# First-layer aggregation products moved into the build of the adjacency, one per step, with six PSUM banks for the steps

## The reference

```python
# layer 0: attention-like, with a sigmoid weight per edge
Q, K, V = h @ w_q, h @ w_k, h @ w_v                     # 8 heads of 16
scores = sum(Q[src] * K[dst], per head) * SCALE * sigmoid(sum(edge_attr))
out = segment_sum(V[dst] * scores, dst) / max(count(dst), 1)
x = x + out @ w_o + b_o
# layer 1: x + relu(segment_sum(h[src], dst) @ W_rel.T + b + h @ W_root.T)
# layer 2: two rounds with segment_sum(h[src] * edge_weight, dst), then a linear map
# layer 3: attention with a softmax over the edges of each destination
```

## Time and profile before

| | |
|---|---|
| median of three runs | 7598.0 us (7587.34 to 7602.8) |
| the profiled execution, its span | 7610.71 us, 7608.9 us |
| TensorE busy | 5794.5 us, 76% |
| VectorE busy | 3770.1 us, 50% |
| ScalarE busy | 2412.7 us, 32% |
| GpSimd busy | 1974.2 us, 26% |
| layer products, line 1117 | 19208 records, 2256.2 us |
| step products, line 1082 | 14112 records, 1924.2 us |
| ScalarE's copies, line 922 | 4704, 1657.8 us |
| VectorE's line 1548 | 2352, 1648.9 us |
| stores adj<-field | 882 of 800 KB, 5.1 us to landing |
| loads field<-adj | 196 of 3200 KB, 10.0 us to landing |

### The profile page before, as it was taken

One profiled execution on the slowest core, in us unless ns is written; L12 is line 12 of the kernel. 1 busy time (PEld: TensorE's weight loads), 2 busy tenths in 40 slices (PEclk: granted clock), 3 DMA queues, 4 the chain that ended last, 5 costly groups with the idle time before them and its releaser, 6 DMA issues.

```text
span 7608.9 us, 163268 instructions
## 1 busy us (share of the span) xinstructions
PE 5794.5 (76%) x48472; PEld 4915.9 (65%) x48472; DVE 3770.1 (50%) x7617; ACT 2412.7 (32%) x7276; POOL 1974.2 (26%) x1782
## 2 busy tenths in 40 slices
PE   1777777777777779999999999996256565556665
PEld 1555555555555569999999999996234444444444
DVE  6899999999999962221111111112143333333333
ACT  2666666666666641111110000002022222122222
POOL 2000000000000000000000000003777777777772
PEclk9899899999989989999999999997677777777776
DMA  6666666766766787676676666672222222222221
GB/s 192 278 282 279 282 276 279 288 276 276 285 275 277 285 291 271 258 277 259 276 278 276 277 278 276 278 279 68 49 56 55 55 55 58 56 55 56 55 55 32
DMA packets 260966, 1542.23 MB, mean 203 GB/s; under 512 B 56235, under 2 KB 86965, under 8 KB 233836
## 3 DMA queue, kind: packets, MB, share of 16 engines
q1 hardware_dynamic: 201380, 1406.77, 47.2%
q0 software_dynamic: 59008, 129.85, 7.1%
q10 hardware_dynamic: 130, 0.80, 0.0%
HBM read 795.75 MB, written 743.08 MB: 202 GB/s over the span
## 4 chain that ended last, share of the span: by engine, by line
PE 51%; DVE 20%; issue 11%; POOL 7%; ACT 4%; ACTq 3%; DMA 2%; DVEq 0%; SPq 0%; POOLq 0%
PE psum L1117 29%; DVE field L1548 11%; PE psum L1082 7%; POOL field L809 7%; PE psum L1284 5%; PE psum L1306 5%; ACT field L922 2%; ACTq L907 2%; ACT field L1013 1%; DVE field L1541 1%; DVE work L1843 1%; DVE work L1847 1%; DMA field<-head_table,cmp 1%; DVE field L1542 1%; PE psum L1304 1%
## 5 line engine op out<-in xcount | busy, mean ns | idle before, releaser
L1117 PE MATMUL psum<-field 128*128 128x128 f32 x19208 | 2256.2, 277 | 24.6 <-issue 19.1
L1117 PEld LDWEIGHTS psum<-field 128*128 128x128 f32 x19208 | 2233.3, 189 | 25.3 <-issue 20.2
L1082 PE MATMUL psum<-field 128*128 128x200 bf16 (+1 forms) x14112 | 1924.2, 281 | 132.8 <-DVE field L1548 114.9
L922 ACT COPY field<-psum x4704 | 1657.8, 416 | 958.8 <-PE psum L1082 665.2
L809 POOL DMA_INDIRECT field<-head_table,cmp x1563 | 1644.7, 1052 | 476.7 <-issue 456.8
L1548 DVE TENSOR_TENSOR field<-field 128x1176 bf16<-128x1176 bf16 x2352 | 1648.9, 761 | 0.0
L1082 PEld LDWEIGHTS psum<-field 128*128 128x128 bf16 x14112 | 1077.2, 101 | 425.7 <-issue 159.1
L1073 PE MATMUL psum<-zero_b 128*128 128x2 bf16 x4704 | 807.6, 172 | 456.2 <-ACT field L922 447.8
L1073 PEld LDWEIGHTS psum<-zero_b 128*128 128x128 bf16 x4704 | 478.4, 102 | 643.5 <-issue 578.9
L753 POOL DMA_INDIRECT field<-tile_rows,step_t_i x74 | 201.2, 2719 | 2405.7 <-PE psum L1053 2355.4
L1013 ACT COPY field<-psum x1611 | 433.6, 269 | 1029.6 <-PE psum L1306 718.6
(11 more groups left out here) (289 smaller groups left out, 2720.0 us busy)
## 6 DMA issues: line engine op xcount, KB each, us to landing
adj<-field SPq DMA_DIRECT2D x882, 800.0 KB, 5.1
field<-adj SPq DMA_DIRECT2D x196, 3200.0 KB, 10.0
field<-head_table,cmp POOLq DMA_INDIRECT x1563
field<-in_edge_attr SPq DMA_DIRECT2D x4, 3072.0 KB, 28.5
head_table<-field SPq DMA_DIRECT2D x7, 476.0 KB, 3.2
tile_rows<-field SPq DMA_DIRECT2D x1, 3328.0 KB, 21.0
right_edges<-zeros SPq DMA_DIRECT2D x1, 3328.0 KB, 19.9
place_rows<-right_edges SPq DMA_DIRECT2D x25, 128.0 KB, 2.8
```

The costliest lines, as they stand in the source:

```text
L922: act.copy(evac[:, :, bass.ds(place, SEG)], build_banks[:, bass.ds(bank, NSEG * SEG)].rearrange("p (w c) -> p w c", w=NSEG)).then_inc(pair ...
L1082: mm = pe.matmul(build_banks[:, bass.ds(cur[j % ROUND], end - first)], hot, pr[:, first:end], start=False, stop=True, skip_group_check=True)
L1117: mm = pe.matmul(ps_y[slot][:, 0:D], source[:, hi, :], adj_in[slot][:, :, 2 * hi:2 * hi + 2], start=(hi == 0), stop=(hi == NB - 1))
```

## The change

- The aggregation of layer 0, Y = A h, is taken apart from the rest of the layer. Behind step 14 + hi of chunk c (c from 26 on, hi from 0 to 48) TensorE does one product of block c - 26: `sum_part`. This goes for all whole chunks, so for blocks 0 to 46; blocks 47 and 48 follow the build.
- The sum needs a bank of its own, `ps_y0`: the steps have six banks, and at an even step TensorE waits for copies up to the second-last step. The products of the two count columns go to the same bank.
- Each array is kept as two of 50 columns (block columns 0 to 24; 25 to 48 and the two count columns): a round is stored by six transfers of half the size. SP loads half 1 of a block behind a chunk's first round, half 0 of the next block behind its third. The halves go to the first 25 blocks of X, which are loaded again from the input later, and to the work buffer.
- ScalarE copies a block's sums to Y at the end of the chunk. Y takes H2's place; H and H2 are exchanged.
- The loads of `src_t` and `dst_t` come after the last step instead of at the beginning.
- The rest of layer 0 is `finish()`: in seven groups of seven blocks instead of block by block.
- The later layers load a block in two transfers. L1's third load waits for the stored tables and for all blocks of `finish()`.

```diff
-BUILD_BANKS = 7
+BUILD_BANKS = 6
+TAB_BANK = 7
+L0_CHUNK = 26
+L0_LOOP = L0_CHUNK // PER_LOOP
+Y_FIRST = 14
...
+            def load_half(b, h):                                   # SP
+                at = b * HALF_COLS + HALF
+                rows_d = adj[SIGMOID * HALVES2 + h]
+                sp.wait_ge(half_summed[h], b + HALF0)
+                sp.dma_start(half_flat[h], rows_d[:, at:at + HALF_COLS] ...).then_inc(half_loaded[h], 16)
...
-                        for i in range(NSEG):
-                            sp.dma_start(adj[i].rearrange("p (s c) -> p s c", c=SEG)[:, bass.ds(base[r], ROUND), :]
+                        for i in range(ARRAYS):
+                            sp.dma_start(adj[i].rearrange("p (s c) -> p s c", c=HALF)[:, bass.ds(base[r], ROUND), :]
...
+                        if summing and rc == 0:
+                            load_half(chunk - L0_CHUNK, 1)
+                        if summing and rc == 2:
+                            load_half(chunk - (L0_CHUNK - 1), 0)
...
+            sp.wait_ge(half_summed[0], BLOCKS + HALF0)
+            sp.dma_start(X[:, 0:X_SPOILT, :], x[0:X_SPOILT * P, :].rearrange("(b p) f -> p b f", p=P)).then_inc(x_reloaded, 16)
...
+            pool.wait_ge(step_added, BSTEPS + ADDED0)              # GpSimd: src_t, dst_t only now
...
+            def copy_sums(b):                                      # ScalarE
+                act.wait_ge(half_summed[1], b + (1 + HALF0))
+                act.copy(one(Y, b), ps_y0).then_inc(y_copied, 1)
...
+                    if at == CHUNK - 1 and summing:
+                        copy_sums(k * PER_LOOP + (slot - L0_CHUNK))
...
+            def sum_part(b, hi):                                   # TensorE
+                h, at = half_of(hi)
+                if hi == 0:
+                    pe.wait_ge(y_copied, b + DONE0)
+                if at == 0:
+                    pe.wait_ge(half_loaded[h], b * 16 + 16)
+                mm = pe.matmul(ps_y0[:, 0:D], H[:, hi, :], half_in[h][:, :, at:at + 2], start=(hi == 0), stop=(hi == NB - 1),
+                               skip_group_check=True)
+                if hi == NB - 1:
+                    for i in range(2):
+                        mm = pe.matmul(ps_y0[0:BPAIRS, D + i:D + i + 1], half_in[h][:, :, HALF - 2 + i], ones[:, 0:1], start=True, stop=True)
+                if hi == NB - 1 or half_of(hi + 1)[0] != h:
+                    mm.then_inc(half_summed[h], 1)
...
                     mm.then_inc(step_added, 1)
+                    if summing and slot * CHUNK + CHUNK <= n and Y_FIRST <= at < Y_FIRST + NB:
+                        sum_part(k * PER_LOOP + (slot - L0_CHUNK), at - Y_FIRST)
...
+            def finish():                                          # TensorE; turn: 7 transposes of H, queries: 7 products Y W_q,
+                ...                                                # values: 7 products with W_k and 7 with W_v
+                turn(0)
+                queries(0)
+                values(0)
+                for g in range(GROUPS):
+                    pe.wait_ge(fin_vs_ready, g + 1)
+                    for j in range(GROUP):
+                        mm = pe.transpose(cols(ps[0], j), cols(fin_vs, j), ident[:, :])
+                    mm.then_inc(fin_turned, 1)
+                    pe.wait_ge(fin_turn_copied, 2 * g + 2)
+                    for j in range(GROUP):
+                        mm = pe.matmul(cols(ps[1], j), cols(fin_vsT, j), W["o"], start=True, stop=True)
+                    mm.then_inc(fin_products, 1)
+                    if g + 1 < GROUPS:
+                        turn(g + 1)
+                        values(g + 1)
+                        queries(g + 1)
+                pe.wait_ge(fin_out_taken, GROUPS)
+            for hi in range(NB):
+                sum_part(BLOCKS - 2, hi)
+            pe.wait_ge(y_copied, BLOCKS - 1 + DONE0)
             tables()
-            blocks_of(L0)
+            for hi in range(NB):
+                sum_part(BLOCKS - 1, hi)
+            finish()
             starts()
...
+            finish()                                               # VectorE: per group scores (4 operations, 3 of 128x896), then
+                                                                   # sums (2 of 128x896, 7 bn_stats, 7 bn_aggr), then scale
```

More of the change, by code:

```diff
@@ L30 @@
 NSEG = 3
+HALVES2 = 2
+HALF = SEG // HALVES2
+HALF_HI = HALF // 2
+ARRAYS = NSEG * HALVES2
 ROUND = 16
@@ L91 @@
 PASSES = 2
-L0, L1, L2A, L2B = range(4)
-LAYER_SEG = (SIGMOID, COUNTED, WEIGHTED, WEIGHTED)
-LAGS = (2, 1, 1, 1)
+L1, L2A, L2B = range(3)
+LAYER_SEG = (COUNTED, WEIGHTED, WEIGHTED)
+LAGS = (1, 1, 1)
+LAYERS = 3
 CRING = 3
@@ L956, in body @@
                         stage_block(0, 0)
-                    if layer == L0 and 1 <= j <= NB:
-                        act.wait_ge(kvq_ready, n)
-                        act.copy(kv[ring(layer, j, 1)], ps_kv).then_inc(kv_copied, 1)
                     if j < NB:
@@ L974, in body @@
                         stage_block(b + 1, j + 1)
-                    if layer == L0 and 1 <= j <= NB:
-                        act.wait_ge(vs_turned, n)
-                        act.copy(vsT[ring(layer, j, 1)], ps_v).then_inc(vsT_copied, 1)
                 over_blocks(act, layer, body)
-            for layer in range(4):
+            finish()
+            for layer in range(LAYERS):
                 blocks_of(layer)
-            act.wait_ge(hT_copied, 4 * NB + DONE0)
+            act.wait_ge(hT_copied, LAYERS * NB + DONE0)
             act.wait_ge(block_written, 2 * NB)
@@ L1034, in _ @@
             pe.sem_inc(y_summed, SUMMED0)
+            for h in range(HALVES2):
+                pe.sem_inc(half_summed[h], HALF0)
             pe.wait_ge(consts, CONSTS)
@@ L1229, in _ @@
+            for hi in range(NB):
+                sum_part(BLOCKS - 2, hi)
+            pe.wait_ge(y_copied, BLOCKS - 1 + DONE0)
             tables()
-            blocks_of(L0)
+            for hi in range(NB):
+                sum_part(BLOCKS - 1, hi)
+            finish()
             starts()
-            for layer in (L1, L2A, L2B):
+            for layer in range(LAYERS):
                 blocks_of(layer)
@@ L1370, in _ @@
             c.then(dve.tensor_scalar(tri[:, :], iota[:, :], pidx[:, 0:1], None, ALU.is_gt))
-            c.then(dve.memset(build_banks, 0.0))
+            c.then(dve.memset(psum[:, :], 0.0))
             dve.wait_ge(loaded_edges, 16 * 9)
@@ L1658, in output @@
                     dve.wait_ge(o_ready, m + 1)
-                    if layer == L0:
-                        c.then(dve.tensor_tensor(one(X, b), one(X, b), ps_o, ALU.add))
-                        dve.sem_inc(o_taken, 1)
-                        c.then(dve.tensor_tensor(one(X, b), one(X, b), bias["o"][:, :], ALU.add))
-                        normalise(c, m, norm_b[s], b)
-                    elif layer == L1:
+                    if layer == L1:
                         c.then(dve.tensor_tensor(lin[s], ps_o, bias["rel"][:, :], ALU.add))
@@ L1704, in body @@
                     n = b + layer * NB
-                    if layer == L0 and 1 <= j <= NB:
-                        scores(c, n, b - 1, ring(layer, j, 1))
                     if lag <= j:
```

346 lines of the change are left out of this document (227 added, 119 removed).

## The result

The changed kernel takes 7652.0 us (median of four runs, 7649.3 to 7662.3) against 7592.8 for the kernel before beside it (four runs, 7587.3 to 7602.8): 1.0078 times, 95% interval 1.0066 to 1.0091. It is slower, by 0.8%, clear of the spread of the runs; 7294 was forecast, with a range of 7200 to 7470. The traces differ by 38.5 us and the medians by 59: the profiled execution of the kernel before lies 18 us above its median.

The account below looks back on a forecast made before the run. The prediction took TensorE to bound the layers and VectorE the build. Saving 478 us at the layer, adding 169 for the build and 5 for six banks, gave -304: 7294 us from a median of 7598.0, range 7200 to 7470.

Parts of the forecast that it names:

- Bound: Whole kernel: layers bound by TensorE, build by VectorE (92% busy), with an idle fifth of TensorE for the moved products.
- A pass of two chunks, after: Build loop with products: 78.7 us a pass, 39.4 a chunk, 3.6 more than before; 47 chunks make +169 us.
- upper bound of 46.8 us a chunk: Build chunk with products at 0.38 us each: 49 x 0.146 more, +517 us in all.
- Product: Each summing product moved into the build takes TensorE 0.234 us, as in the later layers; bounds nothing and 0.38.
- Six banks: Build steps with six banks for seven: copies waited for one later, +5 us, range 0 to 112.
- The DMA queue: Build: 13.1 MB a chunk takes 31.1 us of 39.4 at 422 GB/s, so half loads and stores stay hidden.
- rival 2: Build: transfers become the pace through late stores, 43.8 us a chunk, +207 us, 7501 us in all; chance 0.13.
- The layer: Last build step to next layer's first product: 187 us for 665, saving 478; finish() 18 us a group; bounds 150 and 240.
- X reload: Between build and next layer: a late reload of X, 1.6 MB, adds 5 us.
- Three layers for nothing: The three layers behind: two loads per block for one cost nothing, as their TensorE is full.
- Rival 4: Build: stalls keep TensorE's clock low through half the product stretch, 12.8 us a chunk, +600, 7894 us; chance 0.07.
- Rival 5: Build: chunk 10.1 us longer instead of 3.6, products near 0.36 us, giving back all saved, 7598 us; chance 0.02.

Follow-up runs that it names:

- e6_act_one: Changed kernel with one chunk per loop pass instead of two on TensorE and ScalarE, in chunks with and without products; 7397.8 us, 0.9753 of the kernel before.
- e13_one_no_products: e6_act_one without the build's 47 x 49 summing products, loads kept; one run, no ratio given, a pass of two chunks 79.5 us.
- e15_late_x: e6_act_one with one half's buffer moved to the last half of X, its reload waited for before the fourth group of finish(); 0.9783 of the kernel before.
- e5_one_chunk: Changed kernel with one chunk per pass instead of two in TensorE's summing loop only, all products kept; 0.9990 of the kernel before.

## Why the prediction was wrong

**Bound.** Right: the layers were TensorE's, the build VectorE's, and TensorE's idle fifth could be used. What I read as one stall for ScalarE was a fetch of ScalarE's instructions, and so a thing that grows with traffic.

**A pass of two chunks, after: the step that failed.** 78.7 us forecast, 89.4 measured; 47 chunks made +416, not +169. Of the 17.7 us more than before:
- 4.5 are fetches: 89.4 - 81.2 = 8.2 us a pass in the changed kernel, 71.7 - 68.0 = 3.7 before. In both, steps at the low clock behind the stall are part of it (clock 0.95, and 0.99 with short loops). I had kept the 3.8 of the earlier trace rows and never asked whether TensorE's body still stayed where it was after 49 more products a chunk. It didn't: 8.26 us, beside ScalarE's.
- 13.2 are the work itself, 68.0 to 81.2 with short loops, where 7.1 were forecast. 98 x (0.600 - 0.569) = 3.0 of the difference is the product: 0.26 us and not 0.234. The distance of its columns doesn't explain that and its neighbours at most in part; it stays open. The other 3 I can't divide. The transfers aren't seen in them, as half the loads take nothing off; but relieving TensorE alone helps no more, for without any product a pass still takes 79.5 us.

The upper bound of 46.8 us a chunk was mis-added: 39.4 + 49 x 0.146 is 46.5, and +504 us. The measured 44.6 lies below it; the range, which ended at 7470, stopped short of both.

The Trainium skill (Advanced Engine Details and Errata, ISA Cache) gives TensorE's instruction cache as 128 KB and the other engines' as 32 KB, in lines of 16 KB. The traces agree with these sizes: with the long bodies a pass brought TensorE nine packets of 16 KB, 147 KB, and ScalarE five of 8 KB, 41 KB; halved, an estimated 74 and 21 KB, the bodies weren't fetched at all (no packet from 1200 to 2600 us in e6_act_one). In the size of a packet the trace agrees for TensorE (1.47 MB/90 = 16 KB) and not for ScalarE (0.48 MB/59 = 8 KB). No run shows at which length fetching starts.

**Product.** 0.234 taken, 0.26 measured, within the bounds of 0 and 0.38.

**Six banks.** 5 taken, some 17 left for them in the chunks without products, none with short loops.

**The DMA queue, "hidden".** Wrong, but not by itself decisive: rival 2's mechanism shows once the products are gone, and hardly with them. It gave 43.8 us for a chunk paced by stores; without products the chunk took 43.1, or 39.7 with short loops. That a queued load would fill a store's start-up didn't hold: 13.1 MB in 39.7 us are 330 GB/s, with the engines 91% busy, where I had reckoned with the 422 of the earlier trace rows. That row is of stores alone. The Trainium skill's limit of about 358 GB/s for a core (DMA: Bandwidth & Descriptors, Specifications), weighed in the prediction and set aside, was the better guide for stores and loads together: no window of 1500 us with both passes it. In windows of 2 us the trace of e13_one_no_products does, with up to 419 GB/s.

**The layer.** Right: 201.7 us against 187, with 20.5 us a group of finish() for 18 (two of VectorE's sums start at 3322.78 and 3343.30). The X reload took 31.3 us where 5 were added, and cost little by luck: e15_late_x shows that only some 5 us of the wait stood alone.

**Three layers for nothing.** Wrong: +90.4 us. I had asked whether their second load was hidden, and it is; the operand's distance, 50 floats for 100, I hadn't asked about at all. Had only this failed, the forecast would still have had its sign (-304 + 90); had only the build failed (+254 in the table), it would have kept it too, with -50. It took both.

**Rival 4, the clock.** It didn't come: 0.95 over the product chunks, above the 0.91 of the earlier trace rows. In the product chunks the clock is low behind the jump's stall, and with short loops it reads 0.99. In the kernels without products, where TensorE idles more, it reads 0.82 and 0.87: e13_one_no_products falls to 0.53 or less five times between 1904 and 1984 us, behind idle times of up to 2.3 us, and e6_act_one not once. The rule of the Trainium skill that stood behind this rival (TensorE: Matmul & The Clock Gate, "A second HAM failure mode: psum-queue depth-cycling") agrees with these kernels and says nothing against the changed one, whose products fill the idle times.

**Rival 5** had the right outcome for a wrong reason: a chunk is 8.9 us longer, 2.3 us of it by fetches and 6.6 by products and transfers, with a product of 0.26 us and not 0.36; and the layers gave the rest away.

## What to carry to other kernels

Before you put work into a loop, count what its body becomes on each engine, and look in the DMA queues for instruction packets inside the loop: where there are some, or a wait for "issue" at the first instruction of a pass, the jump has a price that grew here with the body and with the traffic, and a shorter body can be worth more than the change (here the change alone lost 0.8%, short bodies alone gave 1.6%, both together 2.5%). When an operand moves to another layout, price every later use of it, its stride too. And when two resources each stand near their limit (TensorE 93%, DMA 91%), relieving one alone shows little.

## What the runs showed of the hardware

- A loop body that was too long was fetched again in every pass: TensorE's in nine packets of 16 KB, ScalarE's in five of 8 KB. TensorE's stall at the jump was 8.5 us at most with the changed kernel's traffic and 6.0 with one load fewer a chunk; ScalarE's was 6.4 before and 10.2 with the loads and no products. Bodies half as long fetched nothing, with the jump twice as often (e5_one_chunk, e6_act_one).
- An f32 product of 128 columns read in pairs took 272 ns a record at 48 and 64 floats between the pairs, 276 to 277 at 100 and 60, 281 at 56, 283 at 50 and 298 at 52.
- Stores alone ran at 422 GB/s in a window of 2 us; stores and loads together at 334 GB/s over 1500 us, with the engines 91% busy, and in windows of 2 us with the engines full at 275 (2044 to 2046 us of e13_one_no_products) to 419 (2040 to 2042).
- Without the products TensorE's clock read 0.82 and 0.87, with them and short loops 0.99.
